# One split sooner, the routed half first, and a layer's entry by halves

## The reference

```python
# layer 2, second branch: 8 experts of width 128, the best 2 of each token, and a shared part
x1 = silu(einsum('td,ehd->teh', xf, w_gate))
x3 = einsum('td,ehd->teh', xf, w_up)
expert_out = einsum('teh,edh->ted', x1 * x3, w_down)
routed = einsum('te,ted->td', comb, expert_out)
shared = (silu(xf @ sh_gate.T) * (xf @ sh_up.T)) @ sh_down.T
x = x + attention_2 + routed + sigmoid(xf @ se_gate_w.T) * shared
# layer 3, first branch, xn = layernorm(x)
q, k, v = (xn @ W.T + b for W, b in ((Wq, bq), (Wk, bk), (Wv, bv)))
g = sigmoid(xn @ Wg.T + bg)
y = q * cumsum(k * v, axis=1) * g
```

## Time and profile before

| | before |
|---|---|
| three runs, us | 949.98, 953.13, 953.71 |
| the profiled execution's own time, us | 949.16 |
| its span from the first to the last instruction, us | 947.4 |
| mean granted TensorE clock, of full speed | 0.944 |
| TensorE busy, share of the span | 89% |
| last expert and shared products (up to the first down product) | 765 to 828 us |
| down products | 828 to 866 us |
| entry of layer 3, up to the first product with `W3q` | 866 to 900 us |

### The profile page before, as it was taken

The page is one execution under the profiler, slowest core; times in us unless marked ns, Lnnn a source line. Parts: engine busy times, 40 slices in busy tenths (PEclk is TensorE's granted clock), DMA queues, the critical chain, the costliest instruction groups (busy, mean ns, idle before and its releaser), DMA issues.

```text
span 947.4 us, 12031 instructions
## 1 busy us (share of the span) xinstructions
PE 842.4 (89%) x4835; PEld 498.2 (53%) x4835; DVE 558.1 (59%) x993; ACT 391.2 (41%) x478; POOL 228.7 (24%) x208
## 2 busy tenths in 40 slices
PE   9979989889989999986799989679998899697998
PEld 4545443444355344344388776323332278597877
DVE  4967667775774876214343543867775248934451
ACT  3732435445454554653603312135565744401240
POOL 4731313311231025221101104101111257500110
PEclk9879999999999999997899989769999989898999
DMA  6572257418332910204000023955000051000001
GB/s 183 97 260 33 90 106 130 112 45 144 58 100 60 212 49 1 76 1 156 1 0 1 1 93 99 169 73 64 2 1 1 24 210 45 1 1 1 0 1 45
DMA packets 35584, 64.99 MB, mean 69 GB/s; under 512 B 6164, under 2 KB 14908, under 8 KB 35460
## 3 DMA queue, kind: packets, MB, share of 16 engines
q1 hardware_dynamic: 34952, 64.08, 28.6%
q10 hardware_dynamic: 576, 0.13, 0.1%
HBM read 44.35 MB, written 16.29 MB: 64 GB/s over the span
## 4 chain that ended last, share of the span: by engine, by line
PE 64%; DVE 21%; ACT 5%; DMA 3%; SPq 3%; POOL 2%; issue 2%; ACTq 0%; DVEq 0%; POOLq 0%
PE psD L1645 11%; PE psO L1766 10%; DVE mx L1246 10%; PE psA L1645 9%; PE psD L1711 8%; PE psO L1645 8%; PE psA L1729 7%; PE psA L1728 4%; SPq L504 3%; DVE hid_low L1559 2%; PE psD L1713 2%; ACT Pr L937 1%; PE psA L1677 1%; PE psO L1917 1%; PE psD L1777 1%
## 5 line engine op out<-in xcount | busy, mean ns | idle before, releaser
L1246 DVE TENSOR_REDUCE mx<-psD 128x1 f32<-128x512 f32 (+3 forms) x418 | 259.0, 658 | 99.8 <-PE psD L1713 70.4
L937 ACT ACTIVATE Pr<-psA 128x1024 f32<-128x1024 f32 (+3 forms) x192 | 162.0, 866 | 171.9 <-PE psA L1729 171.4
L805 POOL TENSOR_SCALAR_AFFINE_SELECT Pr<-Pr 128x512 f32<-128x512 f32 x96 | 61.2, 637 | 395.4 <-ACT Pr L937 316.8
L942 ACT ACTIVATE Pr<-psA 128x1024 f32<-128x1024 f32 (+3 forms) x96 | 63.3, 702 | 62.8 <-PE psA L1729 62.5
L1766 PE MATMUL psO<-Pr,Vh 128*32 128x512 f32 (+3 forms) x768 | 80.2, 497 | 3.2 <-POOL Pr L805 2.6
L1728 PE MATMUL psA<-Qr,Kr 128*128 128x512 f32 (+3 forms) x192 | 74.8, 403 | 3.8 <-DMA Qr<-mrow 3.8
L1713 PE MATMUL psD<-maskq,identb 128*128 128x128 bf16 x350 | 70.2, 225 | 0.0
L1711 PE MATMUL psD<-Kg,Qs 96*128 96x512 bf16 (+3 forms) x192 | 55.9, 332 | 12.8 <-DVE mx L1246 8.3
L1729 PE MATMUL psA<-Qr,Kr 113*128 113x512 f32 (+3 forms) x192 | 65.9, 349 | 0.0
L1711 PE MATMUL psD<-Kr,Qr 80*128 80x512 bf16 (+3 forms) x166 | 53.8, 349 | 5.5 <-DVE mx L1246 4.0
L1711 PE MATMUL psD<-Ks,Qs 96*128 96x512 bf16 (+3 forms) x166 | 53.4, 351 | 4.6 <-DVE mx L1246 3.9
(11 more groups left out here) (413 smaller groups left out, 1710.1 us busy)
## 6 DMA issues: line engine op xcount, KB each, us to landing
Qr<-d_qr SPq DMA_DIRECT2D x18, 512.0 KB, 11.5
d_qr<-WB SPq DMA_DIRECT2D x9, 512.0 KB, 3.1
Pr<-d_cb SPq DMA_DIRECT2D x8, 512.0 KB, 7.1
Qs<-d_gq SPq DMA_DIRECT2D x24, 128.0 KB, 3.9
Qs<-d_q SPq DMA_DIRECT2D x24, 128.0 KB
Ks<-d_k SPq DMA_DIRECT2D x24, 128.0 KB
Qr<-d_qn SPq DMA_DIRECT2D x18, 128.0 KB, 6.7
Kr<-d_kn SPq DMA_DIRECT2D x18, 128.0 KB, 7.3
```

Of the source, the lines that this page charges most:

```text
L805: pool.affine_select(out=block_, in_=block_, pattern=[[0, GH], [1, P]], compare_op=ALU.is_ge, fill=0.0, base=0, channel_multiplier=-1).the ...
L937: act.activation(place[:, h, q0:T], src[:, q0:T], ACT.Exp, scale=score_scale(i)).then_inc(a_drained, 1)
L942: act.activation(place[:, h:h + 2, q0:T], src[:, :, q0 - HALF:HALF], ACT.Exp, scale=score_scale(i)).then_inc(a_drained, 1)
L1246: dve.tensor_reduce(mx[:, j, part, h0:h0 + nh], src, AX, ALU.max).then_inc(d_drained, 1)
```

## The change

It has three parts.

1. *The split of expert 7.* ScalarE cuts its `hid_high` one unit sooner, behind that of expert 6, with a wait for expert 7's gated product. VectorE subtracts its `hid_low` ahead of the last two gated products and not behind them. GpSimd's `w3m_low` waits for all eight splits.
2. *The down products.* The first pair begins with the routed unit (as before) and waits for the last gated products only ahead of its shared unit; the other three pairs have the shared unit first and the routed unit last. VectorE adds in the same order.
3. *Layer 3's entry by halves of the tokens.* The first four tiles are transposed, both groups of features into one A unit, behind the third pair of down products; ScalarE and VectorE cut and subtract them there, VectorE straight from PSUM (the copy to `xnT` is gone). Behind the last down product TensorE does 18 products of the first half (k, v and v), then transposes the last four tiles, then does the same three for the second half. All else of the 96 products follows, in the order k, g, q, g, q.

```diff
 # GpSimd
             pool.wait_ge(w3m_cut, 1)
+            pool.wait_ge(hid2_split, E)
             pool.tensor_tensor(w3m_low[:], w3m, w3m_high[:], ALU.subtract).then_inc(w3m_split, 1)
 # ScalarE
-                if m >= DC:
+                if DC <= m <= E:
                     act.activation(hid2_high[:, m - DC, :], slot(Qs, m - DC), ACT.Copy).then_inc(hid2_cut, 1)
+                if m == E:
+                    act.wait_ge(d_drained, DU["gsum"] + 2 * E)
+                    act.activation(hid2_high[:, E - 1, :], slot(Qs, E - 1), ACT.Copy).then_inc(hid2_cut, 1)
...
-            std()
-            srcs = []
-            for c in range(DC):
-                srcs.append(take())
-                act.activation(xn_high[:, c, :], srcs[c], ACT.Copy).then_inc(high3_ready, 1)
-            for c in range(DC):
-                act.activation(xnT[:, c, :], srcs[c], ACT.Copy).then_inc(a_drained, 1)
+            for half, pieces in ((0, (0, 1, 2)), (1, (3,))):
+                std(chosen=pieces)
+                src = take().rearrange("p (c t) -> p c t", c=DC)
+                act.activation(xn_high[:, :, half * HALF:(half + 1) * HALF], src, ACT.Copy).then_inc(high3_ready, 1)
 # VectorE
+                if m == E + 1:
+                    hidden2_low(E - 1)
                 for half in range(2):
                     gated_up(slot(Qs, m) if m < E else slot(Ks, m - E), gate[:, m % 2, :], half)
-                if m >= DC:
...
+                if DC <= m <= E:
+                    hidden2_low(m - DC)
...
             for u in range(NT // 2):
-                add_down(u)
-                dve.wait_ge(d_drained, n[0])
...
+                for add in (add_down, add_shared) if u == 0 else (add_shared, add_down):
+                    add(u)
+                    dve.wait_ge(d_drained, n[0])
                 stats((2 * u, 2 * u + 2))
                 norm((2 * u, 2 * u + 2))
+                if u == 2:
+                    transformed_low(0)
+            transformed_low(1)
 # TensorE
-            pe.wait_ge(d_drained, DU["up2"])
             for u in range(NT // 2):
...
+                for terms in (routed, shared) if u == 0 else (shared, routed):
+                    if u == 0 and terms is shared:
+                        pe.wait_ge(d_drained, DU["up2"])
+                    down(u, terms)
+                if u == 2:
+                    transposed_half(xn, 3 * NT, 0, a_unit())
...
+            second = a_unit()
+            key, (v00, v01, v10, v11) = a_unit(), [d_unit() for _ in range(4)]
+            pe.wait_ge(high3_ready, 1)
+            pe.wait_ge(a_drained, A["xnT3"] - 1)
+            by_half(key[:, 0:HALF], 1, 0, 0)
+            by_half(v00, 2, 0, 0).then_inc(d_filled, 1)
+            by_half(v10, 2, 1, 0)
+            transposed_half(xn, 3 * NT, 1, second)
+            for chunks in ((0, 1, 3, 4), (2, 5)):
...
+                k_op = by_half(key[:, HALF:T], 1, 0, 1, chunks)
+                if 2 in chunks:
+                    k_op.then_inc(a_filled, 1)
+                c0 = by_half(v01, 2, 0, 1, chunks)
+                c1 = by_half(v11, 2, 1, 1, chunks)
+            c0.then_inc(d_filled, 2)
+            c1.then_inc(d_filled, 1)
```

More of the change, by code:

```diff
@@ L1568, in _, with add_shared @@
             at("up2")
-            for u in range(NT // 2):
-                add_down(u)
-                dve.wait_ge(d_drained, n[0])
+            def add_shared(u):
                 src = take().rearrange("p (j d) -> p j d", j=2)
@@ L1678, in transposed @@
                     op.then_inc(a_filled, 1)
+            def transposed_half(src, ready, half, dst):
+                for j in range(half * NT // 2, (half + 1) * NT // 2):
+                    pe.wait_ge(xn_ready, ready + j + 1)
+                    for c in range(DC):
+                        at_ = c * HALF + (j % (NT // 2)) * P
+                        op = pe.transpose(dst[:, at_:at_ + P], src[:, j, c * P:(c + 1) * P], identf[:])
+                op.then_inc(a_filled, 1)
             def value_units(lhsT, rhs, chunks, logits=None):
@@ L2061, in _ @@
             pe.wait_ge(a_drained, A["oT2"])
-            pe.wait_ge(d_drained, DU["up2"])
-            for u in range(NT // 2):
[L2064 to L2077, removed]
+            routed = lambda t: ([(fT[:, k, t], w_o2[:, k, :]) for k in range(DC)]
+                                + [term for e in range(E) for w in (ed_high[e // (E // 2)][:, e % (E // 2), :],)
+                                   for term in ((hid2_high[:, e, t], w), (hid2_high[:, e, t], ed_low[:, e, :]),
+                                                (hid2_low[:, e, t], w))])
+            shared = lambda t: [(slot(Ks, m)[:, t], w_sd[:, m, :]) for m in range(DC)]
+            for u in range(NT // 2):
+                for terms in (routed, shared) if u == 0 else (shared, routed):
[4 more added lines that the diff above has]
+                    transposed_half(xn, 3 * NT, 0, a_unit())
             pe.wait_ge(w3_in, 16 * N_W3)
@@ L2083, in _, with by_half @@
             w3 = lambda n, c: (lambda k: (w3m_high, w3m_low, w3m_high)[k % 3][:, n * DC + k // 3, c * P:(c + 1) * P])
-            for first, second in ((1, 2), (3, 0)):
-                for c in range(DC):
-                    if first == 1 and c == 0:
-                        dst = a_unit()
-                        for chunks in ((0, 1, 3, 4), (2, 5)):
-                            if 2 in chunks:
-                                pe.wait_ge(low3_ready, DC)
-                            for half in range(2):
-                                cs = slice(half * HALF, (half + 1) * HALF)
-                                op = product(dst[:, cs], [(w3(first, c)(k), parts3(k, cs)) for k in chunks],
-                                             start=0 in chunks, stop=2 in chunks)
-                        op.then_inc(a_filled, 1)
-                    else:
-                        features(w3(first, c), parts3, range(3 * DC))
-                    for half in range(2):
-                        features_half(w3(second, c), parts3, half, range(3 * DC))
+            def by_half(dst, n, c, half, chunks=range(3 * DC)):
+                cs = slice(half * HALF, (half + 1) * HALF)
+                return product(dst, [(w3(n, c)(k), parts3(k, cs)) for k in chunks], start=0 in chunks, stop=2 in chunks)
@@ L2100, in _ @@
+            c0.then_inc(d_filled, 2)
+            c1.then_inc(d_filled, 1)
+            features(w3(1, 1), parts3, range(3 * DC))
+            for c in range(DC):
+                features(w3(3, c), parts3, range(3 * DC))
+                for half in range(2):
+                    features_half(w3(0, c), parts3, half, range(3 * DC))
             pe.wait_ge(quantised, 1)
```

19 lines of the change are left out of this document (10 added, 9 removed).

## The result

The changed kernel takes 940.73 us (median of four times, 939.94 to 942.83), the kernel before 953.42 on the same chip (four times, 949.98 to 959.29). The medians differ by 12.7 us. The ratio is 0.985, with a 95% interval of 0.9815 to 0.9884: faster, by 11 to 18 us. (A ratio here is an estimate from all times of both kernels, and can differ a little from the quotient of the two medians, 0.9867.) The forecast was 938.7 and a gain of 12.8.

What follows compares the result with a forecast made beforehand. TensorE, busy 89% of the span, bounds the kernel; change pays where it stands still or is clocked low. 5.4 + 0.8 + 6.6 = 12.8 us off 951.5 gives 938.7 us; 8-in-10 range 935.0 to 943.5.

Steps and rivals of the forecast that it cites:

- The first place: TensorE's idle ahead of the first down product, 820 to 828 us: that product starts 5.4 us sooner.
- 4.2 for the collision and 1.2 for the order: Same gap: 4.2 us from hid_low not stalling beside w3m_low, 1.2 us from splitting ahead of the two gated products.
- What is queued behind: VectorE's gated products and quantising instructions beside w3m_low: even if stalled they end by 829.2, under the routed unit until 829.6.
- The price for TensorE without the new order: At the first down products: without the routed part first, TensorE would wait 1.3 us more for the last gated product.
- The clock: Behind the shortened 2.4 us gap ahead of the down products: a fall costs 1.50 us, not 2.30; 0.8 us less.
- the gap is longer than both, so I take the fall: The 2.4 us gap exceeds gaps of 2.07 us (no fall) and 1.91 us (fall), so a 1.50 us fall was assumed.
- the rival without the fall: Clock stays up behind the gap ahead of the down products: 1.5 us more gain, 937.2 us; chance 0.20.
- The down products: Same in number; the first half's eight transposes, moved ahead of the last down product, cost 1.1 us there.
- The second place: Layer 3's entry: from E (last down product issued) to first W3q product 25.9 us, not 33.6; net gain 6.6 us.
- The new wait: Ahead of layer 3's first product: TensorE waits for VectorE's last add, until 1.1 us past the last down product's issue.
- That the halves would not overlap: Rival at layer 3's entry: a wait isn't met, gain there nothing or about 0.4 us, time 945; chance 0.05.
- that the clock would fall here: Rival at layer 3's entry: the clock falls, price 2.4 us, time 941.1; chance 0.13.

Runs made afterwards that it cites:

- e2: Changed kernel without part 1: expert 7's split behind the last two gated products again, GpSimd without the added wait; 947.08 us, ratio 0.9929 to the kernel before.
- e3: Kernel before with one line more: GpSimd's w3m_low waits for all eight splits; 946.11 us, one time only.
- e4: Changed kernel without GpSimd's added wait for all eight splits; 941.32 us, ratio 0.9854 to the kernel before.
- e8: Changed kernel with the wait for the last gated products put back ahead of the first routed unit; 949.55 us, one time only.
- e1: Changed kernel without part 3: layer 3 entered as before, sixteen transposes behind the last down product and the copy; 948.54 us, ratio 0.9919 to the kernel before.
- e5: Changed kernel asking for the value products' fourth PSUM bank (v11) only behind the second eight transposes; 946.22 us, one time only.
- e7: Changed kernel with the routed unit first in all four pairs of down products; 940.63 us, one time only.
- e11: Repeat of e5, the changed kernel with the late v11 bank; 940.33 us, ratio 0.9847 to the kernel before.
- e10: The changed kernel measured again, unaltered; 941.15 us, ratio 0.9846 to the kernel before.
- e9: Kernel before with 30 spare products on TensorE, results unread, in the gap ahead of the down products; 950.82 us, ratio 0.9964.
- e6: Changed kernel with the late v11 bank and expert 7's split moved earlier still, ahead of the rounding of weights; 935.74 us, ratio 0.9811 to the kernel before.
- e12: Repeat of e6, late v11 bank and expert 7's split earlier still; 938.92 us, ratio 0.9831 to the kernel before.

## Why the prediction was right, and where it was not

**The first place, forecast 5.4, measured 5.39** (7.87 - 2.48). The cut is there 6 us ahead of its reader, `hid_low` begins 1.0 us behind TensorE's last product as reckoned, and e2 takes all of it away. The division into 4.2 for the collision and 1.2 for the order is right as a sum and as far as the wait alone goes (e3: 4.28), but the prediction credits the wait with something that the order gives by itself (e4). The rows had it: `hid_low` would end at 822.11, and `w3m_low` started at 821.95.

**What is queued behind.** The two gated products did not stand still beside `w3m_low` (0.68 us each); the `tensor_scalar` behind them did, 3.76 us for what takes 0.34 to 0.35 otherwise. It lay under the routed unit, as forecast. The price for TensorE without the new order, forecast 1.3, was 1.2 (e8). The Trainium skill (SBUF — State Buffer, Who interferes with whom) has both: a VectorE instruction with at most one input in SBUF, outside its two-port modes, doesn't contend with GpSimd, while `tensor_scalar` may. The trace agrees.

**The clock, forecast 0.8, measured 2.2: the term that was mis-sized.** The step that failed was "the gap is longer than both, so I take the fall". In seven profiles with a gap of 2.46 to 2.48 us (the changed kernel twice, e1, e4, e5, e7, e11) the clock fell in two, e1 and e7, at 1.55 and 1.60 us, and stayed in five. My price was right and my choice wrong; the rival without the fall deserved more than its 0.20. The Trainium skill (TensorE: Matmul & The Clock Gate, Part 1) says that the switching point shifts from run to run, and these seven agree, with a fall in two. The same holds at the 1.91 us gap of the earlier trace rows: it was followed by a fall in seven of the fourteen profiles, and the same kernel gave both: in e10 it fell and in the changed kernel's first profile, at 919.57, it did not. But between gaps of about 2 us length isn't what decides: the other gap of the earlier trace rows, 2.07 us, stood in all fourteen profiles and was followed by a fall in none. The prediction set these two side by side by their length, and took from them that a longer gap is likelier to bring a fall; that was the flaw. What sets the one place apart from the other stays open. Where it fell behind the 1.91 us, the price was 1.5 too: 44.2 us from the first `W3q` product to the end of TensorE's work in e10, 42.7 in the first.

**The down products** gave back 0.88 us for the first eight transposes (859.99 - 859.11 in starts, forecast 1.1).

**The second place, forecast 6.6, measured 6.6.** From E to `W3q` 26.0 us against 25.9 forecast, so 33.6 - 26.0 - 0.9 = 6.6 to 6.7. The new wait ends 1.3 us past E (870.39 - 869.08; forecast 1.1), the second transposes start 5.6 past E (5.3) and don't wait, the wait behind them is 1.11 (1.25), and no clock falls. That the halves would not overlap, or that the clock would fall here, showed in no profile. What the prediction doesn't say is how much of this term is the clock. The waits shrank from 3.34 + 2.12 to 1.15 + 1.11 us, by 3.2. Before, ten transposes took 2.51 us where six at full speed took 0.82, which makes 1.37 for ten, and twelve products took 5.18 in place of 2.80: 1.1 + 2.4 = 3.5 us of low clock. So by this estimate about half of the 6.6 us is a fall of the clock that doesn't come any more. It came in all four profiles with the old entry (before, e1, e3, e9), whose first wait was 3.2 to 3.3 us, and in none of the ten with the new one. How much of the shorter second wait is the halving and how much the copy that is gone, no run here separates.

**The sum** of the stage was forecast at 12.8 and is 14.2, all of the difference the clock. **The whole time** was forecast 2.0 us too low, and not by the gain: I took 951.5 us as the base, the mean of four times, while the 41 times of the three later sets have medians of 954.3 to 955.8. 955 - 14.2 would have been 941. The two errors, 3.5 in the base and 1.4 in the clock, went against each other: that the forecast of the time came within 2 us is in part luck, and so is it that the result's medians differ by just the forecast gain (12.7), since the four times before scatter over 9 us.

## What to carry to other kernels

When two engines collide, see what starts each: moving the victim a microsecond ahead of the other's earliest start did the work of a wait, and more. Give a stall of TensorE two prices, its length and the low clock behind it. The second was a matter of chance and place in this kernel for gaps of 1.91 to 2.48 us, and came every time at 3.08 us and more; look it up in several profiles of the same place, and don't carry it over from another gap of the same length. A single profiled execution gives durations, not the level of the whole time: take the level from as many runs as there are, and compare stages from the last event that both kernels share.

## What had not been expected of the hardware

- Whether the clock falls behind a gap of about 2 us depends on the execution and on the place: it fell in 7 of 14 profiles at 1.91 us, in 2 of 7 at 2.46 to 2.48, in none of 14 at 2.07, and in none of 2 at 1.48 and 1.56. The same kernel gave both at 1.91 us (changed and e10, e6 and e12). It fell every time at the longer gaps looked at: a gap of 3.08 us at 563 in before (all 14 profiles), the 3.2 to 3.3 us at the old entry (4 of 4), and 3.59 us and more ahead of the down products (before, e2, e3, e8), where it cost 1.5 to 2.5 us.
- Part of TensorE's work can be shielded from it by work that nobody needs: 30 spare products turned a half unit of 5.97 us into one of 3.75 (e9, one profile), with the first down product 0.1 us later.
- Stretches that no edit touched scattered far more than the total: their end lay anywhere from 819.87 to 832.53 us. The time at the low clock up to 815 us goes with it (granted clock 0.95 on the mean in the earliest, 0.93 in the latest but one); which is cause and which effect was not tried here.
- VectorE beside one GpSimd subtraction of 4.5 us: a subtraction of two SBUF operands, a `tensor_scalar` and a `scalar_tensor_tensor` stood still until it ended (5.42 for 1.22, 3.76 for 0.34, and in e3 4.66 for 0.48), a product with an operand in PSUM ran through in 0.68. And in e4 a subtraction that had begun 1.06 us ahead of GpSimd's took its usual 1.22.
